# Delta attention and latent attention: two value tiles convolved inside the block join, half of the key weighting on ScalarE, and the turned copy ahead of the exponentials

## The chip, the cores and the metric

The kernel runs on one core of one Trainium2 chip. The metric is the device time of one execution in microseconds (us), the median of several runs. Smaller is better.

## The reference

Twelve sublayers in four layers, each `x = x + sublayer(layernorm(x))`, on `x` of shape 4 x 256 x 256 (batches, tokens, features) in float32. Two kinds bear on this change.

The **latent attention** (`L1_xattn`, `L2_xattn`, `L3_xattn`), 16 heads of 256 queries over 512 keys a batch:

```python
scores = jnp.einsum('bhsr,bhlr->bhsl', q_r, k_r)
attn = jax.nn.softmax(scores, axis=-1)
ctx_c = jnp.einsum('bhsl,bld->bhsd', attn, kv_r)
```

The **delta attention** (`L2_attn`). Queries, keys (8 heads) and values (16 heads), 128 wide, come from one projection, a causal convolution over four tokens and a SiLU; queries and keys are scaled to length one. Then, token by token, with a state `Sm` of 128 x 128 a head:

```python
Sm = Sm * a_t[..., None, None]
kv = jnp.einsum('bhk,bhkv->bhv', k_t, Sm)
u = (v_t - kv) * b_t[..., None]
Sm = Sm + k_t[..., None] * u[:, :, None, :]
o = jnp.einsum('bhk,bhkv->bhv', q_t, Sm)
```

## The kernel before

Each engine has its own instruction queue, written out by hand, and runs it in order. Engines wait for each other by semaphores: `pe.wait_ge(*conved.at(n))` holds TensorE's queue until VectorE has counted `conved` up n times. PSUM has 8 banks, `ps[:, bank, :]`, of 512 float32 a partition.

**The latent loops** (lines 1885 to 2033, run three times) have 64 units: a unit is two heads of 128 queries. Each engine walks over steps s; with `LAG = 3`, step s scores unit s and turns unit s - 3.
- TensorE: `scores(s)` (L1912); at odd s `over_keys` (L1934, two finished units times the keys); `turn(s - 3)` (L1922, eight 128 x 128 transposes); at even s `output` (L1944).
- VectorE: `row_max` (L1962), `invert` (L1967), at odd s `keep_sums` (L1980), then `keep` (L1973), which copies the first head's turned weights out of PSUM.
- ScalarE: `exps(s)` (two exponentials, L2010), then `keep(s - 3)` (L2017), the copy of the second head's turned weights.
- GpSimd: divides both heads of a unit by their sums (L2032), in place.

`over_keys(q)` waits for the copies of both heads of units 2q and 2q + 1. `exps` and `scores` share two pairs of PSUM banks: `scores(u)` waits for `exps(u - 2)`.

**The delta attention** (`delta_batches`, L2750) takes the four batches one after another, a batch as two chunks of 128 tokens. Its work comes in 16 tiles n of 2 x 128 channels: keys 0 to 3, queries 4 to 7, values 8 to 15. For each tile TensorE projects (`project`, L2864, into bank `n % 3`), ScalarE multiplies by the last tap (`first_tap`, L3132), VectorE adds three taps (`convolve`, L3284, six instructions), ScalarE applies SiLU (`silu`, L3138). Values are then turned (`turn_values`, L2919) and kept with a scale (`keep_values`, L3144). The values' tiles live in `vT`, four buffers.

The recurrence over a chunk needs the inverse of a triangular 128 x 128 matrix for each head and chunk, 32 in all:
- `keys_keys` (TensorE, L2888) puts key products into banks 4 to 7. `lower` (VectorE, L3312) multiplies them by `gn`, one number a row, and by `decay`, into `inv`: 32 instructions in four groups g.
- DMAs by way of HBM repack the 32 x 32 diagonal blocks into `X`; `solve` (L3328, L3330) inverts them on VectorE; DMAs bring them back.
- `turn_blocks` (VectorE, L3339, six transposes) prepares `J`, which lies over `vT`; GpSimd first clears part of it (L2851), for which the values in `vT` must have been turned.
- The **join** puts the blocks together in two levels on TensorE: `join_first` r = 0, 1 (L2942, L2943), `close_first` r (L2955, L2957, L2959) and `second_level` g = 0 to 4 (L2975, L2979), with copies between them shared by VectorE (L3414, L3418, L3422, L3425) and ScalarE (L3216, L3221, L3223, L3227, L3230).
- Then the values are multiplied by the inverses and the state (from L3071 on).

VectorE's order in a batch: `key_norms`, `lower` 0 to 3, `convolve` 4 to 7, `attend` 0 to 3 (L3321), `convolve` 8 and 9, `solve`, `convolve` 10 to 15, `turn_blocks`, the join's copies, and the rest.

## Time and profile before

| | us |
|---|---|
| median of 3 runs (2892.81 to 2896.42) | 2896.03 |
| the profiled execution | 2889.24 |
| its span in the trace | 2887.4 |
| TensorE busy (share of the span) | 2364.2 (82%) |
| VectorE busy | 1698.7 (59%) |
| ScalarE busy | 1015.2 (35%) |
| GpSimd busy | 769.9 (27%) |
| latent loops, from the first score to the last | 827 to 1053, 1927 to 2152, 2446 to 2671 |
| delta attention, first to last projection | 1220 to 1778 |

The profiled execution's 2889.24 us is the span and 1.8 us around it. Engines overlap, so busy times don't add up to the span; a stage is as long as the engine, or the chain of waits between engines, that leaves no gap in it. In a timeline a bracket names the idle time of the engine just before an instruction and what ended it. An instruction printed as a duration and a count is a merged row: so many instructions from that start.

### The profile page before, as it was taken

The numbers are of one execution on the slowest core, as the hardware profiler recorded it, in microseconds if no ns is written. First come the engines' busy times: TensorE is split into PE (matmuls) and PEld (weight loads), VectorE is DVE, ScalarE is ACT, GpSimd is POOL, SyncE is SP. The second block draws the span as 40 slices with busy tenths as digits, with TensorE's granted clock in tenths as the row PEclk, the third lists the DMA queues.
The fourth block names the chain that finished last, engine by engine and source line by source line (L and its number), as shares of the span: only waits on it lengthen the run. The fifth ranks groups of instructions, "written<-read, shape, count | busy, mean of one in ns | idle before, by whom it ended". The sixth has DMA issues, their size and how long they took to land. (4 is left out here: it accounts for less than half of the span.)

```text
span 2887.4 us, 38148 instructions
## 1 busy us (share of the span) xinstructions
PE 2364.2 (82%) x14562; PEld 1587.5 (55%) x14562; DVE 1698.7 (59%) x3527; ACT 1015.2 (35%) x2336; POOL 769.9 (27%) x573
## 2 busy tenths in 40 slices
PE   6797453348999988878889797889998888999899
PEld 4555322114345555657768586745558665555555
DVE  5435986893445652496969687436656753656311
ACT  3132021651035541135444353435552132555210
POOL 1130001000048862110101010028880000888222
PEclk8689555559999999987979797899999958999999
DMA  1000001002000010220101010210001003000411
GB/s 36 19 21 23 0 0 20 1 23 88 0 1 1 1 51 9 107 57 16 44 16 44 16 45 16 51 52 1 1 1 44 21 6 97 1 1 1 121 38 40
DMA packets 100526, 81.77 MB, mean 28 GB/s; under 512 B 52704, under 2 KB 91857, under 8 KB 99770
## 3 DMA queue, kind: packets, MB, share of 16 engines
q1 hardware_dynamic: 99321, 77.89, 9.5%
q8 instruction: 117, 1.92, 0.3%
q0 software_dynamic: 1024, 1.45, 0.2%
q14 instruction: 64, 0.52, 0.1%
HBM read 73.58 MB, written 5.35 MB: 27 GB/s over the span
## 5 line engine op out<-in xcount | busy, mean ns | idle before, releaser
L2032 POOL TENSOR_SCALAR work<-work,small 128x512 f32<-128x512 f32 x384 | 594.3, 1566 | 706.6 <-DVE small L1967 705.3
L2010 ACT ACTIVATE work<-psum,small 128x512 f32<-128x512 f32 x384 | 260.6, 683 | 254.6 <-DVE small L1962 254.6
L1962 DVE TENSOR_REDUCE small<-psum 128x2 f32<-128x1024 f32 x192 | 234.7, 1224 | 176.0 <-PE psum L1912 176.0
L1922 PEld LDWEIGHTS psum<-consts,work 128*128 128x128 f32 x1536 | 165.5, 141 | 114.0 <-issue 101.8
L1912 PE MATMUL psum<-keysT,arena_a 64*128 64x512 f32 x768 | 219.2, 649 | 8.9 <-ACT work L2010 6.0
L1934 PE MATMUL psum<-work,keys 128*64 128x256 f32 x1536 | 187.0, 384 | 36.6 <-issue 34.2
L1922 PE MATMUL psum<-consts,work 128*128 128x128 f32 x1536 | 211.4, 281 | 3.6 <-DVE work L1973 2.6
L1934 PEld LDWEIGHTS psum<-work,keys 128*64 128x64 f32 x1536 | 120.0, 136 | 136.5 <-issue 110.5
L2864 PE MATMUL psum<-xnT,arena_a 128*128 128x256 f32 x512 | 137.4, 423 | 25.8 <-DVE arena_b L3284 23.8
L1973 DVE COPY work<-psum 128x512 f32<-128x512 f32 x192 | 130.9, 682 | 19.7 <-PE psum L1922 19.5
L2017 ACT ACTIVATE work<-psum 128x512 f32<-128x512 f32 x192 | 114.4, 596 | 71.5 <-PE psum L1922 71.5
L2848 POOL TENSOR_TENSOR work<-arena_b 128x512 f32<-128x512 f32 x32 | 36.2, 1136 | 358.5 <-ACT arena_b L3138 334.7
L2864 PEld LDWEIGHTS psum<-xnT,arena_a 128*128 128x128 f32 x512 | 105.5, 213 | 44.5 <-DVE arena_b L3284 24.9
L2396 PE MATMUL psum<-xnT,arena_b 128*128 128x512 f32 (+1 forms) x272 | 121.8, 602 | 0.0
L1846 DVE TENSOR_TENSOR arena_a<-psum,work 128x512 f32<-128x512 f32 x96 | 58.9, 682 | 82.8 <-PE psum L1811 82.8
L2450 DVE TENSOR_TENSOR arena_a<-arena_a,psum 128x512 f32<-128x512 f32 (+1 forms) x34 | 23.4, 687 | 142.7 <-ACT arena_a L2472 142.7
L1980 DVE COPY work<-psum 128x256 f32<-128x256 f32 x96 | 40.8, 425 | 106.6 <-PE psum L1934 106.6
L261 PE MATMUL psum<-consts,xn 128*128 128x128 f32 x192 | 43.2, 418 | 71.9 <-DVE xn L242 71.9
L1944 PE MATMUL psum<-arena_b,work 128*128 128x256 f32 x384 | 99.1, 381 | 1.6 <-DVE work L1980 1.6
L1912 PEld LDWEIGHTS psum<-keysT,arena_a 64*128 64x128 f32 x768 | 58.9, 186 | 62.4 <-issue 49.5
L1811 PE MATMUL psum<-xnT,arena_b 128*128 128x512 f32 x192 | 86.4, 600 | 1.8 <-PEq L72 1.8
L3284 DVE SCALAR_TENSOR_TENSOR work<-psum,conv_w,work 128x255 f32<-128x255 f32 (+2 forms) x192 | 81.6, 475 | 6.5 <-ACT work L3132 3.9
(585 smaller groups left out, 4777.6 us busy)
## 6 DMA issues: line engine op xcount, KB each, us to landing
arena_b<-alpha_rows SPq DMA_DIRECT2D x16, 512.0 KB, 5.7
arena_a<-in_L_xattn_Wo SPq DMA_DIRECT2D x3, 2048.0 KB, 13.6
arena_a<-in_L_xattn_Wq SPq DMA_DIRECT2D x3, 2048.0 KB, 13.7
arena_a<-in_L_xattn_w_kc_q SPq DMA_DIRECT2D x3, 1536.0 KB, 12.8
arena_a<-in_L_attn_w_qkv SPq DMA_DIRECT2D x1, 4096.0 KB
arena_a<-in_L_xattn_W_qr SPq DMA_DIRECT2D x3, 768.0 KB
arena_b<-in_L_ffn_w_fc SPq DMA_DIRECT2D x1, 2048.0 KB
arena_b<-in_L_ffn_w_proj SPq DMA_DIRECT2D x1, 2048.0 KB
```

Source lines behind the costliest of these rows:

```text
L1811: mm = nc.tensor.matmul(ps[:, u % 2 * 3 + bank, :], Em[:, c, i, col:col + P], xnT[:, c, n * 512:(n + 1) * 512], start=c == 0, stop=c == 1)
L1912: mm = nc.tensor.matmul(ps[:, u % 2 * 2 + j, :], qT[r:r + DC, p, t * P:(t + 1) * P], k.keysT[r:r + DC, b * SK:(b + 1) * SK], start=True, s ...
L1922: mm = nc.tensor.transpose(ps[:, 4 + j, c * P:(c + 1) * P], probs[u % NPB][:, j, c * P:(c + 1) * P], k.c["ident"])
L1934: mm = nc.tensor.matmul(ps[j * DC:(j + 1) * DC, 6, 0:S], k.keys[:, 4 * b + c, :], PT[q % 2][:, j, c], start=c == 0, stop=c == 3)
L1944: mm = nc.tensor.matmul(ps[:, 7, t * D:(t + 1) * D], ctx[q % 2][:, t * P:(t + 1) * P], Bm[:, p, :], start=p == 0 and t == 0, stop=p == HP ...
L1962: nc.vector.tensor_reduce(top[:, 2 * u:2 * u + 2], ps[:, u % 2 * 2:u % 2 * 2 + 2, :], AX.X, ALU.max, negate=True).then_inc(*maxed.up())
L1973: nc.vector.tensor_copy(PT[u // 2 % 2][:, 0, :, u % 2, :], ps[:, 4, :].rearrange("p (c n) -> p c n", c=4)).then_inc(*kept_d.up())
L2010: nc.scalar.activation(probs[u % NPB][:, j, :], ps[:, u % 2 * 2 + j, :], ACT.Exp, bias=top[:, i:i + 1], accum_out=total[:, i:i + 1]).then_ ...
L2017: nc.scalar.activation(PT[u // 2 % 2][:, 1, :, u % 2, :], ps[:, 5, :].rearrange("p (c n) -> p c n", c=4), ACT.Copy).then_inc(*kept_a.up())
L2032: nc.gpsimd.tensor_scalar(probs[u % NPB][:, j, :], probs[u % NPB][:, j, :], total[:, i:i + 1], None, ALU.mult).then_inc(*scaled.up())
L2396: mm = nc.tensor.matmul(ps[0:n_f, 4 + g % 2 * 2 + z, :], gu[:, c, z, i * P:i * P + n_f], xnT[:, c, n * 512:(n + 1) * 512], start=c == 0, s ...
L2864: mm = nc.tensor.matmul(ps[:, n % 3, j * S:(j + 1) * S], w_qkv[:, c, f:f + P], xnT[:, c, b * S:(b + 1) * S], start=c == 0, stop=c == 1)
```

## The change

Three edits.

**Latent loops.** At even s ScalarE's `keep(s - 3)` comes ahead of `exps(s)`; at odd s it stays behind it.

**Weighting.** For g = 2 and 3 `lower` is split. ScalarE multiplies the eight 128 x 128 pieces of a group by `gn` (`weigh_keys`, from PSUM into `inv`); VectorE multiplies the group by `decay` in one instruction of 1024 columns, in place. `convolve(b, 4)` goes between `lower` 2 and `lower` 3. On ScalarE `weigh_keys(2)` stands before `first_tap(4)` and `weigh_keys(3)` behind it, both ahead of the square root.

**Join.** VectorE's `convolve` 14 and 15 move behind `turn_blocks`, one ahead of each copy of `join_first`'s results. Their tiles get the buffer `late`, which lies over `X`, and tile 15 is projected into bank 3. `turn_values` 14 and 15 go to either side of `second_level(0)`; the SiLU and `keep_values` of both go between ScalarE's copies of the join. The join now takes banks 0, 1, 6, 7 alone: `join_first` and `close_first`, which wrote from two places of the array into two banks, write into one bank, at other partitions.

```diff
             for s in range(U + LAG):
+                if s % 2 == 0 and 0 <= s - LAG < U:
+                    keep(s - LAG)
                 if s < U:
                     exps(s)
-                if 0 <= s - LAG < U:
+                if s % 2 == 1 and 0 <= s - LAG < U:
                     keep(s - LAG)
...
+    late = over[:, 3072:4096].rearrange("p (n j s) -> p n j s", n=2, j=2)
...
+        return late[:, n - 14] if n >= 14 else vT[:, (n + 2) % 4]
+
+    def bank_of(n):
+
+        return 3 if n == 15 else n % 3
+
+    def join_bank(g):
+
+        return g if g < 2 else 4 + g
...
-                    pool.wait_ge(*vturned.at(8 * b + 6 + 2 * r))
+                    pool.wait_ge(*vturned.at(8 * b + 4 + 2 * r))
...
-                    nc.tensor.matmul(ps[0:64, 2 * r, o:o + Q], inv_m[0:32, m, 0:64], J[0:32, m, 0:Q], start=True, stop=True)
-                    mm = nc.tensor.matmul(ps[64:128, 2 * r + 1, o:o + Q], inv_m[64:96, m, 64:128], J[64:96, m, 0:Q],
+                    nc.tensor.matmul(ps[0:64, r, o:o + Q], inv_m[0:32, m, 0:64], J[0:32, m, 0:Q], start=True, stop=True)
+                    mm = nc.tensor.matmul(ps[64:128, r, o:o + Q], inv_m[64:96, m, 64:128], J[64:96, m, 0:Q],
                                           start=True, stop=True)
...
-                for n in range(10, 16):
+                for n in range(10, 14):
                     turn_values(b, n)
...
                 close_first(b, 1)
-                for g in range(5):
+                turn_values(b, 14)
+                second_level(b, 0)
+                turn_values(b, 15)
+                for g in range(1, 5):
                     second_level(b, g)
...
+            def weigh_keys(b, g):
+                act.wait_ge(*kkd.at(4 * b + g + 1))
+                if g == 2:
+                    act.wait_ge(*negated.at(b + 1))
+                    if b >= 1:
+                        act.wait_ge(*u1d.at(4 * b))
+                for j in range(2):
+                    for h in range(4 * g + 2 * j, 4 * g + 2 * j + 2):
+                        for c in range(2):
+                            last = nc.scalar.activation(inv[:, h, c * P:(c + 1) * P],
+                                                        ps[:, 4 + g, (2 * j + c) * P:(2 * j + c + 1) * P],
+                                                        ACT.Copy, scale=gn[:, c, h:h + 1])
+                last.then_inc(*weighed.up())
...
+                weigh_keys(b, 2)
                 first_tap(b, 4)
-                act.wait_ge(*normed.at(2 * b + 1))
+                weigh_keys(b, 3)
                 nc.scalar.activation(nk, vs, ACT.Sqrt).then_inc(*rooted.up())
...
             def lower(b, g):
+                if g >= 2:
+                    dve.wait_ge(*weighed.at(2 * b + g - 1))
+                    dve.wait_ge(*scanned.at(8 * b + 2 * g + 2))
+                    nc.vector.tensor_tensor(four(inv, g), four(inv, g), four(decay, g), ALU.mult).then_inc(*lmade.up())
+                    return
...
                 turn_blocks(b, 0)
                 turn_blocks(b, 1)
                 for r in range(2):
+                    convolve(b, 14 + r)
                     dve.wait_ge(*z1d.at(2 * b + r + 1))
```

How the rows of the engines' queues move, at three places (a program prints them; the brackets are the semaphores waited for; lines are those of each version's own file).

ScalarE in a latent loop, from an odd step on. L2010 are the exponentials, L2017 the turned copy. Before, then the change:

```order
L2017 ACTIVATE work<-psum 128x4x128 [waits summed,tposed]
L2010 ACTIVATE work,small<-psum,small 128x512 [waits tposed,maxed]
L2010 ACTIVATE work,small<-psum,small 128x512
L2017 ACTIVATE work<-psum 128x4x128 [waits summed,tposed]
L2010 ACTIVATE work,small<-psum,small 128x512 [waits tposed,maxed]
L2010 ACTIVATE work,small<-psum,small 128x512
```

```order
L2017 ACTIVATE work<-psum 128x4x128 [waits summed,tposed] x2
L2010 ACTIVATE work,small<-psum,small 128x512 [waits tposed,maxed]
L2010 ACTIVATE work,small<-psum,small 128x512
L2010 ACTIVATE work,small<-psum,small 128x512 [waits tposed,maxed]
L2010 ACTIVATE work,small<-psum,small 128x512
L2017 ACTIVATE work<-psum 128x4x128 [waits summed,tposed] x2
```

The two copies now stand together, and the second is ahead of its step's exponentials.

VectorE in a batch, the weighting. Before: L3312 is `lower`, L3284 `convolve(4)`. After: L3365 and L3357 are `lower`, L3331 `convolve(4)`:

```order
L3312 SCALAR_TENSOR_TENSOR work<-psum,work,arena_b 128x128 [waits scanned,kkd]
L3312 SCALAR_TENSOR_TENSOR work<-psum,work,arena_b 128x128 x7
L3312 SCALAR_TENSOR_TENSOR work<-psum,work,arena_b 128x128 [waits scanned,kkd]
L3312 SCALAR_TENSOR_TENSOR work<-psum,work,arena_b 128x128 x7
L3312 SCALAR_TENSOR_TENSOR work<-psum,work,arena_b 128x128 [waits scanned,kkd]
L3312 SCALAR_TENSOR_TENSOR work<-psum,work,arena_b 128x128 x7
L3312 SCALAR_TENSOR_TENSOR work<-psum,work,arena_b 128x128 [waits scanned,kkd]
L3312 SCALAR_TENSOR_TENSOR work<-psum,work,arena_b 128x128 x7
L3284 SCALAR_TENSOR_TENSOR arena_b<-psum,conv_w,arena_b 128x255 [waits first]
L3284 SCALAR_TENSOR_TENSOR arena_b<-psum,conv_w,arena_b 128x255
```

```order
L3365 SCALAR_TENSOR_TENSOR work<-psum,work,arena_b 128x128 [waits scanned,kkd]
L3365 SCALAR_TENSOR_TENSOR work<-psum,work,arena_b 128x128 x7
L3365 SCALAR_TENSOR_TENSOR work<-psum,work,arena_b 128x128 [waits scanned,kkd]
L3365 SCALAR_TENSOR_TENSOR work<-psum,work,arena_b 128x128 x7
L3357 TENSOR_TENSOR work<-work,arena_b 128x1024 [waits scanned,weighed]
L3331 SCALAR_TENSOR_TENSOR arena_b<-psum,conv_w,arena_b 128x255 [waits first]
L3331 SCALAR_TENSOR_TENSOR arena_b<-psum,conv_w,arena_b 128x255
L3331 SCALAR_TENSOR_TENSOR arena_b<-psum,conv_w,arena_b 128x254 [waits chain_dve]
L3331 SCALAR_TENSOR_TENSOR arena_b<-psum,conv_w,arena_b 128x254
L3331 SCALAR_TENSOR_TENSOR arena_b<-psum,conv_w,arena_b 128x253 [waits chain_dve]
L3331 SCALAR_TENSOR_TENSOR arena_b<-psum,conv_w,arena_b 128x253
L3357 TENSOR_TENSOR work<-work,arena_b 128x1024 [waits scanned,weighed]
```

Sixteen instructions of 128 columns became two of 1024, which wait for ScalarE (`weighed`), and the convolution stands between them.

VectorE in a batch, the join. Before: L3284 is `convolve(15)`, L3339 `turn_blocks`, L3414 the copies. After: L3392 is `turn_blocks`, L3331 `convolve(14)`, L3470 the first copy:

```order
L3284 SCALAR_TENSOR_TENSOR work<-psum,conv_w,work 128x255 [waits first]
L3284 SCALAR_TENSOR_TENSOR work<-psum,conv_w,work 128x255
L3284 SCALAR_TENSOR_TENSOR work<-psum,conv_w,work 128x254 [waits chain_dve]
L3284 SCALAR_TENSOR_TENSOR work<-psum,conv_w,work 128x254
L3284 SCALAR_TENSOR_TENSOR work<-psum,conv_w,work 128x253 [waits chain_dve]
L3284 SCALAR_TENSOR_TENSOR work<-psum,conv_w,work 128x253
L3339 STREAM_TRANSPOSE work<-work 32x16x32 [waits cleared,back]
L3339 STREAM_TRANSPOSE work<-work 32x16x32 x2
L3339 STREAM_TRANSPOSE work<-work 32x16x32 [waits cleared,back]
L3339 STREAM_TRANSPOSE work<-work 32x16x32 x2
L3414 COPY work<-psum 64x512 [waits z1d] x2
```

```order
L3392 STREAM_TRANSPOSE work<-work 32x16x32 [waits cleared,back]
L3392 STREAM_TRANSPOSE work<-work 32x16x32 x2
L3392 STREAM_TRANSPOSE work<-work 32x16x32 [waits cleared,back]
L3392 STREAM_TRANSPOSE work<-work 32x16x32 x2
L3331 SCALAR_TENSOR_TENSOR work<-psum,conv_w,work 128x255 [waits first]
L3331 SCALAR_TENSOR_TENSOR work<-psum,conv_w,work 128x255
L3331 SCALAR_TENSOR_TENSOR work<-psum,conv_w,work 128x254 [waits chain_dve]
L3331 SCALAR_TENSOR_TENSOR work<-psum,conv_w,work 128x254
L3331 SCALAR_TENSOR_TENSOR work<-psum,conv_w,work 128x253 [waits chain_dve]
L3331 SCALAR_TENSOR_TENSOR work<-psum,conv_w,work 128x253
L3470 COPY work<-psum 64x512 [waits z1d]
L3331 SCALAR_TENSOR_TENSOR work<-psum,conv_w,work 128x255 [waits first]
```

The transposes now follow `convolve(13)`, and a convolution stands ahead of each copy.

## Rows read from the trace of the kernel before

**Rows 1.** part 1 of the page, busy time of each engine

```profile
PE 2364.2 (82%) x14562; PEld 1587.5 (55%) x14562; DVE 1698.7 (59%) x3527; ACT 1015.2 (35%) x2336; POOL 769.9 (27%) x573
```

**Rows 2.** part 5 of the page, groups by line (busy, mean ns | idle before)

```profile
L1934 PE MATMUL psum<-work,keys 128*64 128x256 f32 x1536 | 187.0, 384 | 36.6 <-issue 34.2
...
L2017 ACT ACTIVATE work<-psum 128x512 f32<-128x512 f32 x192 | 114.4, 596 | 71.5 <-PE psum L1922 71.5
```

**Rows 3.** timeline of one latent loop, 946 to 954 us (start, duration, engine, line)

```profile
946.65 1.13 PE L1912 MATMUL psum<-keysT,arena_a 64*128 64x512 f32 x4
...
947.71 1.09 PE L1922 MATMUL psum<-consts,work 128*128 128x128 f32 x8
...
947.83 1.23 DVE L1962 TENSOR_REDUCE small<-psum 128x2 f32<-128x1024 f32 x1 [0.82 <-PE psum L1912]
...
949.04 0.67 DVE L1973 COPY work<-psum 128x512 f32<-128x512 f32 x1
...
949.09 0.69 ACT L2010 ACTIVATE work<-psum,small 128x512 f32<-128x512 f32 x1 [1.73 <-DVE small L1962]
...
949.22 6.19 POOL L2032 TENSOR_SCALAR work<-work,small 128x512 f32<-128x512 f32 x4 [1.18 <-DVE small L1967]
...
949.60 1.13 PE L1912 MATMUL psum<-keysT,arena_a 64*128 64x512 f32 x4
...
950.43 0.59 ACT L2017 ACTIVATE work<-psum 128x512 f32<-128x512 f32 x1
...
951.12 1.95 PE L1934 MATMUL psum<-work,keys 128*64 128x256 f32 x16 [0.40 <-issue]
...
954.02 1.13 PE L1912 MATMUL psum<-keysT,arena_a 64*128 64x512 f32 x4
```

**Rows 4.** timeline, VectorE, delta batch 1

```profile
1407.07 8.35 DVE L3312 SCALAR_TENSOR_TENSOR work<-psum,work,arena_b 128x128 f32<-128x128 f32 x32
...
1415.34 10.45 DVE L3284 SCALAR_TENSOR_TENSOR arena_b<-psum,conv_w,arena_b 128x255 f32<-128x255 f32 x24
...
1430.33 1.22 DVE L3321 TENSOR_TENSOR arena_b<-arena_b,psum 128x1024 f32<-128x1024 f32 x1 [1.15 <-PE psum L2906]
...
1467.55 2.68 DVE L3284 SCALAR_TENSOR_TENSOR work<-psum,conv_w,work 128x255 f32<-128x255 f32 x6 [0.98 <-ACT work L3132]
...
1475.34 4.28 DVE L3339 STREAM_TRANSPOSE work<-work 32x512 f32<-32x512 f32 x6
...
1481.26 0.68 DVE L3414 COPY work<-psum 64x512 f32<-64x512 f32 x1 [1.65 <-PE psum L2943]
...
1484.68 0.68 DVE L3414 COPY work<-psum 64x512 f32<-64x512 f32 x1 [2.73 <-PE psum L2943]
...
1488.26 0.68 DVE L3418 COPY work<-psum 32x512 f32<-32x512 f32 x1 [1.02 <-PE psum L2959]
```

**Rows 5.** timeline, TensorE, delta batch 1

```profile
1418.07 3.78 PE L2864 MATMUL psum<-xnT,arena_a 128*128 128x256 f32 x8 [6.07 <-DVE arena_b L3284]
...
1462.11 1.12 PE L2919 MATMUL psum<-consts,work 128*128 128x128 f32 x4 [6.81 <-ACT work L3138]
...
1477.60 0.28 PE L2942 MATMUL psum<-work 32*64 32x32 f32 x1 [0.82 <-DVE work L3339]
...
1484.57 0.26 PE L2955 MATMUL psum<-work 32*32 32x32 f32 x1
```

**Rows 6.** timeline, ScalarE, delta batch 1

```profile
1408.47 1.28 ACT L3180 ACT_TABLE_LOAD   x1
...
1469.11 0.84 ACT L3132 ACTIVATE work<-psum,conv_w 128x256 f32<-128x256 f32 x2 [0.35 <-PE psum L2864]
...
1505.53 3.21 ACT L3237 ACTIVATE work<-psum,work 128x128 f32<-128x128 f32 x12 [0.54 <-DVE work L3430]
```

**Rows 7.** timeline, GpSimd and the DMA queue of SyncE, delta batch 1

```profile
1471.97 0.52 POOL L2851 MEMSET work<- 32x512 f32 x1 [44.40 <-PE psum L2919]
...
1418.85 0.34 SPq L2832 DMA_DIRECT2D work<-delta_blocks  x1
```

More of the change, by code:

```diff
@@ L2800, in dest @@
     def dest(n):
-        return qkT[:, 2 * pair(n):2 * pair(n) + 2, :] if n < 8 else vT[:, n % 4]
+        if n < 8:
+            return qkT[:, 2 * pair(n):2 * pair(n) + 2, :]
+        return late[:, n - 14] if n >= 14 else vT[:, (n + 2) % 4]
[3 more added lines that the diff above has]
+        return g if g < 2 else 4 + g
     def four(t, g):
@@ L2856, in project @@
             def project(b, n):
-                if n >= 3:
+                if n == 15:
+                    pe.wait_ge(*normed.at(2 * b + 2))
+                elif n >= 3:
                     pe.wait_ge(*conved.at(16 * b + n - 2))
@@ L2950, in close_first @@
                 if r == 0:
-                    pe.wait_ge(*vkept.at(8 * b + 8))
                     pe.wait_ge(*gated.at(8 * b + 8))
@@ L3064, in _ @@
                 close_first(b, 1)
-                for g in range(5):
+                turn_values(b, 14)
+                second_level(b, 0)
+                turn_values(b, 15)
+                for g in range(1, 5):
                     second_level(b, g)
                 for g in range(4):
+                    if g == 0:
+                        pe.wait_ge(*vkept.at(8 * b + 6))
+                    elif g == 2:
+                        pe.wait_ge(*conved.at(16 * b + 15))
+                    elif g == 3:
+                        pe.wait_ge(*vkept.at(8 * b + 8))
                     pe.wait_ge(*(x2kept if g % 2 == 0 else x2kept_a).at(2 * b + g // 2 + 1))
@@ L3126, in first_tap @@
                 act.wait_ge(*proj.at(16 * b + n + 1))
-                if n >= 12:
+                if n >= 14:
+                    act.wait_ge(*unlaned.at(16 * (b + 1)))
+                elif n >= 12:
                     act.wait_ge(*vturned.at(8 * b + n - 11))
@@ L3131, in first_tap @@
                 for j in range(2):
-                    last = nc.scalar.activation(dest(n)[:, j, :], ps[:, n % 3, j * S:(j + 1) * S], ACT.Copy,
+                    last = nc.scalar.activation(dest(n)[:, j, :], ps[:, bank_of(n), j * S:(j + 1) * S], ACT.Copy,
                                                 scale=conv_w[:, 2 * pair(n) + j, 3:4])
@@ L3206, in _ @@
                     last.then_inc(*scaled_out.up())
-                for n in range(10, 16):
+                for n in range(10, 14):
                     silu(b, n)
@@ L3213, in _ @@
                 for r in range(2):
+                    if r == 1:
+                        silu(b, 14)
                     act.wait_ge(*z1d.at(2 * b + r + 1))
                     ms = slice(16 * r, 16 * r + 16)
-                    nc.scalar.activation(Zs[64:128, ms, :], ps[64:128, 2 * r + 1, :].rearrange("p (m s) -> p m s", m=16),
+                    nc.scalar.activation(Zs[64:128, ms, :], ps[64:128, r, :].rearrange("p (m s) -> p m s", m=16),
                                          ACT.Copy).then_inc(*z1kept_a.up())
+                silu(b, 15)
                 for r in range(2):
@@ L3230, in _ @@
                     nc.scalar.activation(inv_m[0:64, 8 * g:8 * g + 8, 64:128],
-                                         ps[0:64, 4 + g, :].rearrange("p (m s) -> p m s", m=8), ACT.Copy
+                                         ps[0:64, join_bank(g), :].rearrange("p (m s) -> p m s", m=8), ACT.Copy
                                          ).then_inc(*x2kept_a.up())
+                    if g == 1:
+                        keep_values(b, 15)
                 for g in range(4):
@@ L3394, in _ @@
                 key_norms(b)
-                for g in range(4):
+                for g in range(3):
                     lower(b, g)
-                for n in range(4, 8):
+                convolve(b, 4)
+                lower(b, 3)
+                for n in range(5, 8):
                     convolve(b, n)
@@ L3406, in _ @@
                 solve(b)
-                for n in range(10, 16):
+                for n in range(10, 14):
                     convolve(b, n)
```

35 lines of the change are left out of this document (19 added, 16 removed).

## The prediction, made before the changed kernel was run

> **What bounds the kernel now.** I read the page first, then the groups by line, then timelines of one latent loop and one delta batch. TensorE is busy 82% of the span [rows 1], so a stage either has TensorE without gaps or another engine's chain, and the change must be judged stage by stage.
>
> In the groups, the matmuls over keys have 36.6 us of TensorE's idle time just ahead of them, 34.2 of it put down to "issue", that is to nothing the trace names [rows 2]. The latent timeline says what it is [rows 3]. Scores of an even step start at 946.65, of the next even step at 954.02: a pair of units takes 7.37 us. In the even step the transposes start 1.06 us after the scores (947.71). In the odd step the matmuls over keys start 1.52 us after the scores (949.60 to 951.12), with 0.40 idle ahead. They wait for ScalarE's copy of the odd unit, which runs 950.43 to 951.02, ends 0.10 ahead of them, and stood behind two exponentials begun at 949.09, although what it copies was turned by 948.80. TensorE has no other gap in the pair. So the loops are TensorE's work plus one wait for ScalarE.
>
> In a delta batch VectorE sets the pace from the weighting to the block transposes [rows 4]: 32 weightings from 1407.07, four convolutions from 1415.34, then a wait of 1.15 for TensorE, then the solve; convolution 13 runs 1467.55 to 1470.23, the transposes only from 1475.34, since convolutions 14 and 15 lie between. After that TensorE and the copies alternate, and VectorE is idle 1.65 and 2.73 ahead of its two first copies.
>
> **The change, latent loops.** The copy in an even step can start when the transposes end, 948.80, and ends about 949.43. The exponentials then start at 949.43 and not 949.09, 0.34 later. Their next readers have more room than that: VectorE inverts the sums only behind the next row maximum, and the scores that reuse the bank come at 954.02, 3.6 us after the exponentials' end at 950.43. The other copy that the matmuls over keys need, VectorE's, ends at 949.71 [rows 3]. Both copies are thus in before the scores have gone through, and the matmuls can start 1.06 after them as the transposes do: 0.46 us a pair. There are 96 pairs in three loops, less one at the end of each loop with no scores ahead: 93 x 0.46 = 42.8 us. The idle time of the groups (34.2) is the low bound of this term, 96 x 0.46 = 44 the high one. Late next is TensorE itself. GpSimd works 6.19 us a pair [rows 3] and would fill 6.19 of 6.91.
>
> **The change, weighting.** The 32 instructions take 1415.34 - 1407.07 = 8.27 us, 0.26 each; sixteen go, -4.1. Two of 1024 columns come. The nearest row is a product of that size that also reads PSUM, 1.22 us [rows 4]; both operands now lie in SBUF, for which I have no row of this size, so 1.2 each, with 0.6 (twice as fast) and 2.1 (no gain at all over eight small ones) as bounds. Net -1.7 on VectorE.
>
> ScalarE's price is 8 pieces of 128 columns at 3.21 / 12 = 0.27 [rows 6], 2.15 us a group. It is idle when `gn` comes at 1407.1, so group 2 is ready at 1409.3, needed at 1411.2; tap 4 at 1410.1, needed at 1412.4; group 3 at 1412.3, needed at 1415.0. What pays is queued behind: the table load for the square root (at 1408.47 before [rows 6]) moves to 1412.3, and with two copies, tap 5 and the second table load the SiLU of tile 4 comes at about 1417.1, only one microsecond earlier than before. TensorE's projection 7 waits for convolution 4, which now ends at 1415.0 and not 1417.95. In the trace it started at 1418.07 after 6.07 idle and took 3.78 [rows 5], and from there TensorE ran without a gap until the last query-key product, 12.3 us later, for which VectorE waits (1430.33, 1.15 idle [rows 4]). Started at 1415.05 this chain ends near 1427.4, the SiLU at 1417.7 being just in time even if projection 7 takes half of 3.78. VectorE arrives there at 1416.2 + three convolutions (7.8) + three products (3.6) = 1427.6. So the 1.15 goes with the 1.7: -2.8 us a batch. Group 3 is done 0.8 later than before, which moves the fetch of the packed blocks (issued at 1418.85 [rows 7]); the solve, at 1436.7, hides it.
>
> **The change, join.** Convolution 13 still ends at 1470.23. The transposes follow; the second half waits for the clearing that ends at 1472.5 (1471.97 + 0.52 [rows 7], it follows the turning of tile 13 as now), 0.15 us. They end at 1474.7. Then convolution 14 (2.6) to 1477.3, a copy (0.7), convolution 15 to 1480.6, a copy to 1481.3. Tap 14 is there (1469.11 [rows 6]), tap 15 soon after. TensorE starts the join at 1472.4 and not 1477.60; a half takes 1481.2 - 1477.6 = 3.6, so both are done at 1479.7, ahead of VectorE. The second closing starts at 1481.35. In the trace the closings start at 1484.57 [rows 5] and the copy of the second at 1488.26 [rows 4]: 1.8 each, the second at 1486.4. Gain 5.05. Given back: two turnings of values, each at the price of the one at 1462.11, which followed an idle stretch as the join's small matmuls nearly are: 1.12 us [rows 5]. The first is all on the path; the second lies where TensorE waits about 0.75 for a copy anyway, 0.35. The convolutions' and SiLUs' own time is hidden by the join, their copies on ScalarE (0.84 each) stand where it idles. Net -3.6 us a batch, between 0 (if the inserted work fills the join again) and -5.
>
> **Sum.** -42.8 - 4 x (2.8 + 3.6) = -42.8 - 25.6 = -68.4. Against the profiled execution, 2889.24, this gives 2820.8. The median shown is 6.8 above that execution, so I expect a median of 2827.6, say 2827.
>
> **A page against it.** `join_first` starts pairs from two places of the array, 0.28 us long and one pair about every 0.11 us, into two banks; after the change into one [rows 5]. No row shows that. The Trainium skill, page "TensorEngine Tiling (Array Packing)", section "Gotcha 1: PSUM Pressure", says that different row tiles cannot access the same PSUM bank simultaneously. By that rule the pairs would go one after the other, the second rival.
>
> **The rivals.**
> 1. *The join fills up.* The two turnings or the SiLUs come where they hold the chain, and the join gives nothing: 2827 + 14 = 2841. For it: the join is a ping-pong in which every wait counts. Against: each inserted piece has an idle stretch longer than itself but one.
> 2. *One bank, one after the other.* `join_first` takes twice its 7.2, the closings twice 3.6; VectorE covers part of the first. The second closing would end at about 1493.4 and not 1483.1, 10 us a batch: 2827 + 41 = 2868. Against: `close_first` already writes two partition ranges of one bank, though from one place of the array.
> 3. *The wait is not the copy.* If the 0.40 is TensorE's own, as the label says, the loops stay: 2827 + 43 = 2870. Against: the copy's end 0.10 ahead.
> 4. *The copy holds the exponentials: slower.* In the latent loops the exponentials now wait for the turning, which waits for GpSimd. If that circle closes, a pair takes 6.19 + 1.09 + 0.59 + 1.34 (the exponentials, 949.09 to 950.43) and some 0.4 of inversion and hand-overs, 9.6 and not 7.37: 96 x 2.2 = +215, 3085 us with the delta's gain. It decides when GpSimd's results come later than the turning could start. Its first unit of the run from 949.22 is done at 952.3 and turned at 955.08 [rows 3], 2.8 us of slack, 2.3 after the change.
>
> **How the numbers follow.** Forecast 0.73, rival 1 0.09, rival 2 0.06, rival 3 0.07, rival 4 0.03, and 0.02 that gains and losses cancel. A measurement of this kernel can tell 0.2%, about 6 us, from no change. Faster: 0.73 + 0.09 + 0.06 + 0.07 = 0.95; same 0.02; slower 0.03. The range: all bounds at their best give -44 - 4 x (4 + 5) = -80, 2816, less 2 for the runs' spread, 2814; the latent term at its low bound and rival 1 together give 2827 + 8.6 + 14 = 2850. Rivals 2, 3 and 4 lie outside.
>
> **What would show it.** Right: no idle time ahead of the matmuls over keys, a pair of 6.9 us, exponentials 0.3 us later in even steps; no VectorE wait ahead of the last `attend`; a batch some 6 us shorter; transposes straight behind convolution 13. Wrong: a gap of 0.4 still there; pairs of `join_first` 0.2 us apart; GpSimd without idle time in the loops.

## The result, and the profile after it

| | us | runs |
|---|---|---|
| before, median | 2895.59 (2892.81 to 2896.42) | 4 |
| after, median | 2827.48 (2820.67 to 2832.6) | 4 |
| ratio | 0.9765, 95% interval 0.974 to 0.979 | |
| profiled execution after | 2824.04, span 2822.2, mean granted clock 0.868 | |

The median is 68 us less, and 2827 was forecast. That the two agree within 1 us is luck: the four executions of the change lie 12 us apart, and against the sum the loops gave 1.7 us less, the batches 1.8 more, and 3.3 were lost elsewhere. The page of the changed kernel, the busy times and the two groups that answer to [rows 1, 2]:

```profile
PE 2350.7 (83%) x14562; PEld 1560.1 (55%) x14562; DVE 1690.6 (60%) x3471; ACT 1029.7 (36%) x2400; POOL 769.7 (27%) x573
...
L1934 PE MATMUL psum<-work,keys 128*64 128x256 f32 x1536 | 186.9, 385 | 0.0
L2017 ACT ACTIVATE work<-psum 128x512 f32<-128x512 f32 x192 | 114.6, 597 | 161.7 <-PE psum L1922 161.7
```

TensorE's 36.6 us ahead of the matmuls over keys are 0.0. ScalarE's copy has 161.7 us of idle time ahead of it, where it had 71.5: in even steps it now waits for what it copies and no longer stands behind the exponentials. The timeline of one pair, to be laid beside [rows 3]:

```profile
942.14 1.13 PE L1912 MATMUL psum<-keysT,arena_a 64*128 64x512 f32 x4
...
943.20 1.95 PE L1934 MATMUL psum<-work,keys 128*64 128x256 f32 x16
...
946.11 1.13 PE L1912 MATMUL psum<-keysT,arena_a 64*128 64x512 f32 x4
...
948.30 0.60 ACT L2017 ACTIVATE work<-psum 128x512 f32<-128x512 f32 x1 [1.49 <-PE psum L1922]
...
948.67 1.57 POOL L2034 TENSOR_SCALAR work<-work,small 128x512 f32<-128x512 f32 x1 [0.72 <-DVE small L1967]
...
948.79 0.68 ACT L2010 ACTIVATE work<-psum,small 128x512 f32<-128x512 f32 x1
949.06 0.70 PE L1912 MATMUL psum<-keysT,arena_a 64*128 64x512 f32 x2
```

The matmuls over keys follow the scores by 1.06 (942.14 to 943.20) and have no bracket. The pair takes 949.06 - 942.14 = 6.92 us. The exponentials start 2.68 after the even step's scores (946.11 to 948.79); before it was 2.44. GpSimd still works 6.19 a pair and keeps 0.72 idle.

VectorE in delta batch 1 (the batches are counted 0 to 3, as in the rows), which answers to [rows 4]:

```profile
1389.64 4.22 DVE L3365 SCALAR_TENSOR_TENSOR work<-psum,work,arena_b 128x128 f32<-128x128 f32 x16
1393.77 1.22 DVE L3357 TENSOR_TENSOR work<-work,arena_b 128x1024 f32<-128x1024 f32 x1
1394.90 2.68 DVE L3331 SCALAR_TENSOR_TENSOR arena_b<-psum,conv_w,arena_b 128x255 f32<-128x255 f32 x6
1397.50 1.22 DVE L3357 TENSOR_TENSOR work<-work,arena_b 128x1024 f32<-128x1024 f32 x1
1398.63 7.87 DVE L3331 SCALAR_TENSOR_TENSOR arena_b<-psum,conv_w,arena_b 128x255 f32<-128x255 f32 x18
1406.42 2.34 DVE L3374 TENSOR_TENSOR arena_b<-arena_b,psum 128x1024 f32<-128x1024 f32 x2
...
1447.00 2.68 DVE L3331 SCALAR_TENSOR_TENSOR work<-psum,conv_w,work 128x255 f32<-128x255 f32 x6 [0.97 <-ACT work L3158]
1449.60 2.12 DVE L3392 STREAM_TRANSPOSE work<-work 32x512 f32<-32x512 f32 x3
1452.03 2.13 DVE L3392 STREAM_TRANSPOSE work<-work 32x512 f32<-32x512 f32 x3 [0.31 <-POOL work L2865]
1454.19 2.68 DVE L3331 SCALAR_TENSOR_TENSOR work<-psum,conv_w,work 128x255 f32<-128x255 f32 x6
1456.80 0.67 DVE L3470 COPY work<-psum 64x512 f32<-64x512 f32 x1
1457.39 2.66 DVE L3331 SCALAR_TENSOR_TENSOR work<-psum,conv_w,work 128x255 f32<-128x255 f32 x6
1459.97 0.67 DVE L3470 COPY work<-psum 64x512 f32<-64x512 f32 x1
1460.68 0.68 DVE L3474 COPY work<-psum 32x512 f32<-32x512 f32 x1
1462.68 0.68 DVE L3474 COPY work<-psum 32x512 f32<-32x512 f32 x1 [1.32 <-PE psum L2974]
1465.61 0.69 DVE L3478 COPY work<-psum 64x512 f32<-64x512 f32 x1 [2.24 <-PE psum L2990]
...
1478.72 0.69 DVE L3486 TENSOR_TENSOR work<-psum,work 128x512 f32<-128x512 f32 x1 [3.92 <-PE psum L3095]
```

The two 1024-wide products stand on either side of convolution 4, and the last query-key products (1406.42) have no wait ahead. The block transposes stand right behind convolution 13; convolutions 14 and 15 fill what were the waits ahead of the two first copies of the join.

**Where the 65.2 us between the two profiled executions (2889.24 and 2824.04) come from.** A stage is measured between two points that both kernels have. First to last scores of a latent loop, mean of the three: 226.0 us before (the first from 827.2 to 1053.3), 212.3 after (827.2 to 1039.5), so 13.7 a loop, 41.1 in three. From one batch's solve to the next: 153.68 before, 146.82 after (means of three periods), so 6.86 a batch, 27.4 if all four gain as much. Together 68.5; some 3.3 are lost elsewhere, nearly all of it between the first latent loop and the first solve, and the last section says what lies there.

### The profile page after: what moved, and what is told of

It is laid out like the page before. It is cut to its first block and busy times, and to the rows that moved or that the text cites. A ratio compares the mean times of both kernels' runs of the same rounds, so it can differ in the third digit from the quotient of the medians.

```text
span 2822.2 us, 38168 instructions
## 1 busy us (share of the span) xinstructions
PE 2350.7 (83%) x14562; PEld 1560.1 (55%) x14562; DVE 1690.6 (60%) x3471; ACT 1029.7 (36%) x2400; POOL 769.7 (27%) x573
## 3 DMA queue, kind: packets, MB, share of 16 engines
q0 software_dynamic: 1024, 1.45, 0.2%
## 5 line engine op out<-in xcount | busy, mean ns | idle before, releaser
L2010 ACT ACTIVATE work<-psum,small 128x512 f32<-128x512 f32 x384 | 260.0, 684 | 122.9 <-DVE small L1962 122.9
L2017 ACT ACTIVATE work<-psum 128x512 f32<-128x512 f32 x192 | 114.6, 597 | 161.7 <-PE psum L1922 161.7
L1934 PEld LDWEIGHTS psum<-work,keys 128*64 128x64 f32 x1536 | 101.7, 136 | 111.8 <-issue 67.9
L3331 DVE SCALAR_TENSOR_TENSOR work<-psum,conv_w,work 128x255 f32<-128x255 f32 (+2 forms) x192 | 82.3, 475 | 6.6 <-ACT work L3158 3.9
L2398 PEld LDWEIGHTS psum<-xnT,arena_b 128*128 128x128 f32 (+1 forms) x272 | 51.7, 191 | 60.8 <-issue 60.1
## 6 DMA issues: line engine op xcount, KB each, us to landing
arena_a<-in_L_xattn_Wo SPq DMA_DIRECT2D x3, 2048.0 KB, 14.1
```

Source lines behind the costliest of these rows:

```text
L1934: mm = nc.tensor.matmul(ps[j * DC:(j + 1) * DC, 6, 0:S], k.keys[:, 4 * b + c, :], PT[q % 2][:, j, c], start=c == 0, stop=c == 3)
L2010: nc.scalar.activation(probs[u % NPB][:, j, :], ps[:, u % 2 * 2 + j, :], ACT.Exp, bias=top[:, i:i + 1], accum_out=total[:, i:i + 1]).then_ ...
L2017: nc.scalar.activation(PT[u // 2 % 2][:, 1, :, u % 2, :], ps[:, 5, :].rearrange("p (c n) -> p c n", c=4), ACT.Copy).then_inc(*kept_a.up())
L2398: mm = nc.tensor.matmul(ps[0:n_f, 4 + g % 2 * 2 + z, :], gu[:, c, z, i * P:i * P + n_f], xnT[:, c, n * 512:(n + 1) * 512], start=c == 0, s ...
```

## The experiments

Each was run five or six times beside the kernel before, whose median was 2891 to 2896 us; the one-bank kernel ran once. The latent loop (mean of three) and the batch period (mean of the three from solve to solve) are read from each run's own trace.

| run | median us | ratio to before, 95% | latent loop us | batch period us |
|---|---|---|---|---|
| the copy alone | 2845.94 | 0.9848 (0.9827 to 0.987) | 212.3 | 153.8 |
| the weighting alone | 2875.42 | 0.9946 (0.9928 to 0.9964) | 225.9 | 150.55 |
| the join alone | 2876.82 | 0.9948 (0.9928 to 0.9968) | 226.0 | 150.16 |
| the change | 2827.48 | 0.9765 (0.974 to 0.979) | 212.3 | 146.82 |
| copy ahead in every step | 2824.41 | 0.9773 (0.9754 to 0.9791) | 212.1 | 146.79 |
| one bank, nothing else | 2889.71 (once) | - | 225.9 | 153.83 |
| turnings one product later | 2813.34 | 0.9718 (0.97 to 0.9736) | 212.3 | 143.72 |
| projection 13 first | 2828.94 | 0.9767 (0.9752 to 0.9782) | 212.4 | 146.79 |
| both of these | 2815.37 | 0.9714 (0.9697 to 0.9732) | 212.3 | 142.44 |
| turnings together | 2812.9 | 0.9732 (0.9712 to 0.9752) | 212.4 | 144.61 |
| turnings two later | 2819.51 | 0.974 (0.9718 to 0.9761) | 212.3 | 143.95 |

### The three parts alone

The copy alone: the kernel before, and

```diff
+                if s % 2 == 0 and 0 <= s - LAG < U:
+                    keep(s - LAG)
...
-                if 0 <= s - LAG < U:
+                if s % 2 == 1 and 0 <= s - LAG < U:
                     keep(s - LAG)
```

> The kernel before with the latent edit alone (in even steps ScalarE copies the turned weights ahead of the exponentials). Theory (the 0.40 us gap ahead of the matmuls over keys is ScalarE's copy): a pair of units takes 6.9 us and not 7.37, 93 pairs x 0.45 = 41 us, so about 2854 us. Rival (the gap is TensorE's own): 2895 us, the gap still there. Rival (parts help each other): less than 36 us of gain here.

Measured: 45.5 us less, with an interval from 38 to 50, which leaves out both rivals. The group of the matmuls over keys has lost its idle time, as in the whole change:

```profile
L1934 PE MATMUL psum<-work,keys 128*64 128x256 f32 x1536 | 186.9, 385 | 0.0
```

The loops are 13.7 shorter and the batch period stays (153.8 against 153.7): this is the latent term, and nothing else of the change is in it.

The weighting alone: `weigh_keys` on ScalarE, the two 1024-wide products on VectorE, the second of them behind convolution 4; the join as before.

```diff
-                for g in range(4):
+                for g in range(3):
...
-                for n in range(4, 8):
+                convolve(b, 4)
+                lower(b, 3)
+                for n in range(5, 8):
```

> The kernel before with the weighting edit alone. Theory: VectorE reaches convolution 13 about 3.1 us earlier in each of four batches, as in the trace of the change, whatever the join does: 12 us, so about 2883 us. Rival (the gain is only the 1.7 us of VectorE work, the wait for the last query-key product stays): 7 us, 2889 us. Rival (the later square root and table loads on ScalarE cost what VectorE saves): 2895 us.

Measured: 16 us less, with an interval from 10 to 21, which leaves out both rivals. The trace gives 153.68 - 150.55 = 3.13 a batch, 12.5 in four. In the loops the wait is where it was:

```profile
L1934 PE MATMUL psum<-work,keys 128*64 128x256 f32 x1536 | 186.9, 384 | 36.3 <-issue 34.3 <-ACT work L2017 2.0
```

The join alone: the edits of the change to banks, buffers and order, with the weighting and the copy as before.

```diff
-                for n in range(10, 16):
+                for n in range(10, 14):
...
+                turn_values(b, 14)
+                second_level(b, 0)
+                turn_values(b, 15)
...
+                    convolve(b, 14 + r)
```

> The kernel before with the join edit alone. Theory: from convolution 13 to the first product with the values 3.85 us less in each batch, 15 us, so about 2880 us. Rival (the join gives its gain only because the weighting moved the fetches and TensorE's clock): 2890 us or more. The three gains of these three kernels should add up to the whole change, 68 us, within some 6 us.

Measured: 14.7 us less, with an interval from 9 to 21, which leaves out the rival; by the trace 153.68 - 150.16 = 3.52 a batch, 14.1 in four. The expectation that the three gains add up to 68 within 6 us missed by the medians: 45.5 + 16.1 + 14.7 = 76.3, 8 more. In the stages that were edited they do add up: 41.1 + 12.5 + 14.1 = 67.7 by the traces, against 68.5 for the whole, and 3.13 + 3.52 = 6.65 of the 6.86 a batch. So the parts neither help nor hinder each other there. Some of the 8 us lies where no kernel was edited: the profiled execution of the copy alone reaches its first latent loop at 821.8 us, those of the kernel before and of the change at 827.2.

### The copy ahead of the exponentials in every step

```diff
-                if s % 2 == 0 and 0 <= s - LAG < U:
+                if 0 <= s - LAG < U:
                     keep(s - LAG)
...
-                if s % 2 == 1 and 0 <= s - LAG < U:
-                    keep(s - LAG)
```

> The change with ScalarE's copy ahead of the exponentials in odd steps too. There it waits for transposes that TensorE makes only after the matmuls over keys, so the exponentials start about 2 us later; by the timeline of the change they end some 0.9 us before the scores that reuse their bank. Theory (TensorE sets the pace and that slack holds): within 5 us of the change, 2825 to 2835. Rival (the copy holds the exponentials and the circle through GpSimd closes): over 1 us a pair, 2920 us or more, with GpSimd or TensorE idle in every pair.

Measured: 2824.41, the change's own time within the spread, and loops of 212.1. In odd steps the exponentials now start 4.6 us after their scores (938.02 to 942.59), where it was 2.4, and that costs nothing: the slack on the way from the exponentials through GpSimd back to the turning is more than 2.1 us. That the exponentials wait for the turning, as rival 4 said, is so; that the circle would then set the pace is what no run here shows, since it never closed.

### One bank for two places of the array

The kernel before, with only the banks of the pairs changed (`close_first` and the readers likewise):

```diff
-                    mm = nc.tensor.matmul(ps[64:128, 2 * r + 1, o:o + Q], inv_m[64:96, m, 64:128], J[64:96, m, 0:Q],
+                    mm = nc.tensor.matmul(ps[64:128, 2 * r, o:o + Q], inv_m[64:96, m, 64:128], J[64:96, m, 0:Q],
```

> The kernel before, with one thing changed: the two matmuls of a pair of join_first, which start from two places of the array, write one bank of PSUM and not two, and close_first's likewise. Order and amount of work stay. Theory (one bank costs nothing): the two lines of join_first keep their mean of about 0.28 us and a pitch of about 0.11 us a pair, close_first's pairs keep theirs, the time is that of before within 0.3%. Rival (the rule of the Trainium skill's page on array tiling, that different row tiles cannot access the same bank simultaneously): the pairs go one after the other, the pitch doubles to over 0.2 us, and each half of the join takes some 3.6 us more; four batches give 2890 + 4 x 10 = 2930 us.

Measured: 2889.71 in one execution, against a median of 2894.81 for the kernel before. The trace decides it. First the kernel before, two banks, then this run, one bank (of the second matmul of a pair: how many, min/median/max in ns, first and last start):

```profile
L2943 PE MATMUL psum<-work x256: 289/289/312, 1324.0 to 1791.8; 32*64 32x32 f32 x128
```

```profile
L2943 PE MATMUL psum<-work x256: 289/289/311, 1324.8 to 1793.0; 32*64 32x32 f32 x128
```

And start times at the join's beginning, again the kernel before and then this run:

```profile
1477.70 0.29 PE L2942 MATMUL psum<-work 32*64 32x32 f32 x1
...
1477.80 0.29 PE L2942 MATMUL psum<-work 32*64 32x32 f32 x1
```

```profile
1478.75 0.29 PE L2942 MATMUL psum<-work 32*64 32x32 f32 x1
1478.78 0.29 PE L2943 MATMUL psum<-work 32*64 32x32 f32 x1
1478.85 0.29 PE L2942 MATMUL psum<-work 32*64 32x32 f32 x1
1478.89 0.29 PE L2943 MATMUL psum<-work 32*64 32x32 f32 x1
```

The second matmul of a pair starts 0.03 to 0.04 us behind the first, and a pair comes every 0.10 to 0.11 us, in one bank as in two. The closings do not slow either: from the second copy of the first halves to the first copy of the closings it is 1.87 us in both kernels. So for this form (float32, two places of the array, other partitions of the same bank) nothing goes one after the other as the second rival had it from the rule, and that rival is out. This is a statement on time alone. The Trainium skill's page "PSUM — Partial Sum Buffer", section "PSUM bank collisions raise a hardware error", quotes the broad rule as well, and as measured gives a narrower one: two TensorE writes from different row tiles collide if they share a bank and one of its four 32-partition quadrants. The pairs here write partitions 0 to 63 and 64 to 127, so no run here shows that case, and the result should not be carried to it.

### Two attempts on what is left of the join

In delta batch 1 of the change VectorE still waits 0.97 us ahead of convolution 13, and 2.24 ahead of the second level's first copy, which comes behind the turning of values 14. The turnings moved, the changed kernel otherwise:

```diff
-                turn_values(b, 14)
                 second_level(b, 0)
+                turn_values(b, 14)
+                second_level(b, 1)
                 turn_values(b, 15)
-                for g in range(1, 5):
+                for g in range(2, 5):
```

> The changed kernel, with the turning of values 14 put behind the second level's first product and the turning of values 15 behind its second one, instead of ahead of them. Theory (the turning of values 14 stands on the path, since the second level's first product is what the chain of the join waits for next): 0.5 to 1.1 us a batch come off, so 2 to 4 us in all, 2824 us against 2827. Rival (SiLU and convolution 14 and 15 are then late for the attend products at the end): the same time or up to 4 us more.

The projection of tile 13 moved ahead, with ScalarE's order to match:

```diff
+                project(b, 13)
                 for n in range(10, 14):
                     turn_values(b, n)
-                    if n < 13:
+                    if 11 <= n < 13:
                         project(b, n + 3)
...
-                for n in range(10, 14):
+                silu(b, 10)
+                silu(b, 11)
+                first_tap(b, 13)
+                keep_values(b, 10)
+                keep_values(b, 11)
+                for n in range(12, 14):
```

> The changed kernel, with the projection of tile 13 put ahead of the turning of values 10 on TensorE, and on ScalarE the first tap of tile 13 put ahead of the two copies of values 10 and 11. Before and after, VectorE is idle for 0.97 us ahead of convolution 13, which waits for that first tap. Theory (that wait is the projection's place in the order): the idle time goes, convolution 13 starts 0.97 us earlier, and the batch is shorter by as much: 4 x 0.97 = 3.9 us, 2823 us against 2827. Rival (TensorE's work ahead of the join is the limit, so the join starts as late as before): the gap moves to the first copies of the join, no change.

> The changed kernel with both reorderings, the turnings of values 14 and 15 later and the projection of tile 13 earlier. If the two act at different places they add up: 3 + 4 = 7 us off, about 2820 us. If the join is bound by TensorE's start, only the larger of the two shows, 2823 us. If neither place is on the path, 2827 us.

Measured: 2813.34, 2828.94 and 2815.37. The second attempt does what it should at its place and gives it back at the next:

```profile
1451.95 2.68 DVE L3336 SCALAR_TENSOR_TENSOR work<-psum,conv_w,work 128x255 f32<-128x255 f32 x6
1454.54 2.12 DVE L3397 STREAM_TRANSPOSE work<-work 32x512 f32<-32x512 f32 x3
1457.82 2.13 DVE L3397 STREAM_TRANSPOSE work<-work 32x512 f32<-32x512 f32 x3 [1.16 <-POOL work L2865]
1459.99 2.69 DVE L3336 SCALAR_TENSOR_TENSOR work<-psum,conv_w,work 128x255 f32<-128x255 f32 x6
```

The 0.97 ahead of convolution 13 is gone. But the second half of the transposes waits for GpSimd's clearing, which waits for the turning of tile 13; that one came no earlier, so 0.31 became 1.16. Neither theory nor rival had named this wait.

The run with both, at 2815.37, is below all three times that were expected, since those took the first attempt for 3 us; its median is no better than that of the first attempt alone. By the traces the early projection keeps a little in this company: the batch period is 142.44, against 143.72.

The first attempt gives 3.1 a batch in the mean (146.82 - 143.72), four times the middle of what was expected, and its three periods differ (141.4, 146.2, 143.6) where those of the change are alike (146.9, 146.8, 146.8). From the second closing's copy to the first product after the join, delta batch 1 takes 13.91 us and not the 16.04 of the changed kernel. Of the 2.13, 1.06 lies in the step to the second level's first copy, where the turning of values 14 was. The rest lies in the last two steps, which hold no turning in either kernel. The same stretch in every batch, us:

| run | batch 0 | 1 | 2 | 3 |
|---|---|---|---|---|
| the change | 16.0 | 16.0 | 16.0 | 16.0 |
| turnings one product later | 11.5 | 13.9 | 13.9 | 13.9 |
| both reorderings | 11.5 | 13.9 | 13.9 | 13.9 |
| turnings together (below) | 12.0 | 14.6 | 15.9 | 11.9 |
| turnings two later (below) | 14.8 | 14.5 | 14.4 | 14.4 |

### What the other half is

Two more orders of the same turnings, with nothing else changed: both between the first and second product of the level, and each two products later than in the change.

```diff
-                turn_values(b, 14)
                 second_level(b, 0)
+                turn_values(b, 14)
                 turn_values(b, 15)
```

> The changed kernel with both turnings of values, 14 and 15, between the second level's first and second product. The earlier run with them one product later each gave 2813 us, 12 less than the changed kernel (3.1 us a batch), where 0.75 us a batch was expected. Its trace shows 1.05 us from the place of the turning of values 14, and 1.13 us in the last two steps of the second level, which ran at the full clock and not at half. Theory (the place of turning 14 and the earlier rise of the clock are two effects): the step to the second level's first result stays 1.05 us shorter than in the changed kernel, the next step, which now holds both turnings, is some 0.7 us longer; with the clock back as early as in that run the time is 2813 to 2817 us, with the clock at half until the attend products it is 2824 to 2827 us. Rival (the whole gain is the place of the turnings): last steps as in the changed kernel, and still 2813 us.

```diff
-                turn_values(b, 14)
                 second_level(b, 0)
+                second_level(b, 1)
+                turn_values(b, 14)
+                second_level(b, 2)
                 turn_values(b, 15)
-                for g in range(1, 5):
+                for g in range(3, 5):
```

> The changed kernel with the turning of values 14 behind the second level's second product, that of values 15 behind its third. Theory (each step of the second level ends in a copy for which TensorE waits, so a turning costs least behind the product whose copies take longest): the first two steps of the second level are free of turnings and the time is 2809 to 2815 us if the clock comes back as early as in the run with the turnings one product later. Rival (the values are then late for the attend products): the first attend product for the last two groups waits for the copy of values 15, and the time is 2816 to 2822 us. If the clock stays at half in the second level: 2820 to 2827 us.

Measured: 2812.9 and 2819.51. The run with the turnings together tells most, because its own batches differ. VectorE's copies of the second level up to the first product after it, batch 2 and then batch 3, the same instructions:

```profile
1603.25 0.69 DVE L3478 COPY work<-psum 64x512 f32<-64x512 f32 x1 [1.19 <-PE psum L2990]
1607.09 0.68 DVE L3481 COPY work<-psum 64x512 f32<-64x512 f32 x1 [3.14 <-PE psum L2994]
1609.76 0.69 DVE L3478 COPY work<-psum 64x512 f32<-64x512 f32 x1 [1.99 <-PE psum L2990]
1612.62 0.68 DVE L3481 COPY work<-psum 64x512 f32<-64x512 f32 x1 [2.16 <-PE psum L2994]
1617.22 0.69 DVE L3486 TENSOR_TENSOR work<-psum,work 128x512 f32<-128x512 f32 x1 [3.92 <-PE psum L3095]
...
1749.68 0.69 DVE L3478 COPY work<-psum 64x512 f32<-64x512 f32 x1 [1.19 <-PE psum L2990]
1752.93 0.68 DVE L3481 COPY work<-psum 64x512 f32<-64x512 f32 x1 [2.56 <-PE psum L2994]
1754.78 0.69 DVE L3478 COPY work<-psum 64x512 f32<-64x512 f32 x1 [1.16 <-PE psum L2990]
1756.81 0.68 DVE L3481 COPY work<-psum 64x512 f32<-64x512 f32 x1 [1.34 <-PE psum L2994]
1759.68 0.69 DVE L3486 TENSOR_TENSOR work<-psum,work 128x512 f32<-128x512 f32 x1 [2.19 <-PE psum L3095]
```

Batch 2 takes 13.97 us from its first row to its last, batch 3 takes 10.00. The busy times of the same stretches (columns: window, its length, busy time of TensorE, its weight loads, VectorE, ScalarE and GpSimd with counts, then the granted TensorE clock, share of DMA, GB/s):

```profile
1605.31:1609.31 4.00, 3.23 (x61) 3.07 (x60) 0.68 (x1) 0.59 (x1) 0.00 (x0) 0.50 0.00 0
1609.31:1613.31 4.00, 2.51 (x42) 2.16 (x40) 1.38 (x2) 1.90 (x4) 0.00 (x0) 0.50 0.02 4
...
1751.41:1755.41 4.00, 2.60 (x65) 2.29 (x64) 1.31 (x2) 1.34 (x4) 0.00 (x0) 0.92 0.00 0
1755.41:1759.41 4.00, 3.15 (x56) 2.97 (x57) 0.74 (x2) 1.91 (x5) 0.00 (x0) 1.00 0.01 4
```

Batch 2 ran its second level at a granted clock of 0.50 (1.2 GHz); in batch 3 it was 0.92 and then 1.00 (2.4 GHz). In the changed kernel all four batches run the second level at 0.50.

So there are two effects, as the theory had it, and they can be told apart. The step to the first copy is 1.87 us in all these orders and 2.93 in the change: 1.06 from the place of the turning. How much of it stays depends on where the turning goes. One product later each, the next step is as long as in the change (2.98). With both together it grows to 3.84 (0.86 more, 0.7 was expected), and batch 2, at 0.50 throughout, is only 0.2 us shorter than the change's (15.85 against 16.03). The clock is worth up to 4 us in a batch, and in the run with the turnings together it makes nearly the whole gain; the rival, that the gain is all the place of the turnings, is out.

Why these orders let the clock rise and the change's does not stays open: the batches of one execution differ with the same instructions, and no run here set it at will.

With the turnings two products later the third step takes 4.61 us (2.66 in the change), because ScalarE's copy of values 14 (1472.08 to 1472.92 in delta batch 1) stands ahead of its copy of the second level (1472.94), for which TensorE waits. The time lies in the range of that run's rival, but not by its mechanism: the step to the first product behind the join is the short one (2.87, in the change 4.61). Nor does its trace bear out a loss of 6 us against one product later: the batch period is 143.95 against 143.72, and of the 9 us between the two profiled executions 5.6 lie ahead of the first latent loop, where the kernels are the same.

The version to keep is the one with the turnings one product later: 2813.34 us, ratio 0.9718 (0.97 to 0.9736), below the interval of the change. The one with the turnings together and the one with both reorderings read the same within the intervals, and part of the gain of all three comes from the clock, which differs from batch to batch.

## Why the prediction was right

Point by point, by its own steps:

- **Latent loops: -42.8 forecast, -41.1 by the trace, -45.5 by the run with the copy alone.** Mechanism and place as forecast: the pair went from 7.37 to 6.92. A loop gave 13.7 and not 14.3: the pair gained 0.45 and not 0.46, and 31 pairs of 0.45 would still be 14.0. The exponentials come 0.24 later in even steps, 0.34 was forecast. The label "issue" was ScalarE's copy, as the 0.10 between the copy's end and the matmuls' start had said; rival 3 is out.
- **Weighting: -2.8 forecast, -3.1.** From the first weighting to convolution 13 it was 60.48 us before (1407.07 to 1467.55) and is 57.36 (1389.64 to 1447.00). The 1024-wide product takes 1.22 from SBUF, the same as from PSUM; 1.2 was taken. Group 3 is ready 0.7 later than before (1398.63 - 1389.64 = 8.99, against 8.27), 0.8 was forecast, and the solve hid it. What paid was, as forecast, the queue behind it:

```profile
1397.64 2.77 PE L2880 MATMUL psum<-xnT,arena_a 128*128 128x256 f32 x8 [3.07 <-DVE arena_b L3331]
```

  Projection 7 starts 8.00 after the first weighting (7.98 forecast) with 3.07 of idle time instead of the 6.07 of [rows 5], and takes 2.77 instead of 3.78. VectorE's 1.15 ahead of the last query-key products is gone. The run of this part alone gave the same 3.13 a batch.
- **Join: -3.6 forecast, -3.85.** From convolution 13 to the first product after the join: 35.57 before (1467.55 to 1503.12), 31.72 after. Counted from convolution 13's start, the last copy of the first halves ends at 13.64, where 13.75 was forecast (1481.3 - 1467.55), and the copy of the second closing starts at 15.68; before it was 20.71 [rows 4]. That is the gain of 5.03, with 5.05 forecast. Given back: 16.04 from there to the first product, against 14.86, so 1.18 and not 1.47. The run of this part alone gave 3.52 a batch and not 3.85: another 0.2 goes between the first product and the next batch's weighting (57.5 before, 57.75 in that run). The wait for the clearing was 0.31, 0.15 was forecast.
- **What the sum had wrong without effect.** A half of the join was taken at 3.6 us, the price of [rows 5]. It took 2.05 (1451.87 to 1453.92, delta batch 1): in the change TensorE has run projections and turnings until 0.5 us ahead of the join, which then runs at the full clock. The first row is the kernel before, 1477.60 to 1481.20, the second the change:

```profile
1477.60:1481.20 3.60, 3.60 (x68) 3.60 (x70) 1.99 (x3) 0.06 (x1) 0.00 (x0) 0.50 0.00 0
```

```profile
1452.00:1456.00 4.00, 3.71 (x126) 3.60 (x125) 3.85 (x7) 0.88 (x2) 0.00 (x0) 1.00 0.02 6
```

  VectorE sets the pace there, so nothing came of it. Where TensorE sets it, in the second level, the step that was missing is the one the later runs found: the forecast priced the turning of 14 on the path (1.12, measured 1.06) but took the clock of the second level as given. For the change itself that was no error, since its second level ran at 0.50 as before.
- **The rivals.** 1, the join fills up: no, 5.03 came. 2, one bank: no, by its own run. 3: no, as above. 4: no, the exponentials came 0.24 later and the loops got shorter; even 2.1 later in odd steps they did not close the circle.

## What to carry to other kernels

An idle time labelled "issue" ahead of one line is worth a look at who ended last before it: a producer that stood behind other work in its own queue, on data long ready, can be moved at no cost if the work it is moved past has slack (here 34.2 us of "issue" in [rows 2], gone after the edit). Work that is inserted in a ping-pong of two engines is free only if it stands in the wait of its own engine, and one slot later can be free where one slot earlier is not (the turning of 14 cost 1.06 us ahead of the second level, the next slot 0.12: 2.98 against 2.86 in the kernel before). After an edit removes a wait, the next one can be a small instruction of a third engine, here a clearing of 0.5 us.

## What was not expected of the hardware

- **The clock of a short stretch is no constant of its code.** The same matmuls of the join take 218 ns each in the change, in a stretch at a granted clock of 1.00, and 289 before, at 0.50. The same second level takes 10.0 us or 14.0 in two batches of one execution, at 0.92 to 1.00 and at 0.50.
- **It also takes back.** Of the 3.3 us lost between the stages 2.4 lie in the router's 32 matmuls behind the first latent attention, which the change does not touch. Before they take 4.6 us, a mean of 284 ns; after, 7.0 at 361. The same windows, before and then after:

```profile
1078.00:1084.00 6.00, 4.58 (x32) 4.51 (x32) 0.92 (x4) 1.60 (x2) 0.00 (x0) 0.78 1.09 387
```

```profile
1064.00:1070.00 6.00, 5.59 (x27) 5.62 (x27) 0.09 (x1) 1.28 (x1) 0.00 (x0) 0.50 1.07 379
```

  The granted clock had risen during them before and stayed at 0.50 after. This is not put down to the change: with the copy moved in the latent loop the 32 matmuls take 7.0 us in four profiled executions and 4.2 to 5.0 in four others, with it where it was 4.4 to 5.1 in all four. Whether the order has a part in it stays open, since each kernel was profiled once. The stretch from the start to the first latent loop, the same instructions in all twelve kernels, takes from 821.8 to 837.5 us. A difference of some us between two executions is therefore read stage by stage, as above, and not from the total.
- **Two matmuls from two places of the array into one PSUM bank**, at other partitions, come as fast as into two banks: 289 ns each and a pair every 0.10 to 0.11 us in both.
